# Local attention on one Trainium2 core: mask added by quarters of the array, values weighted right behind the scores, tokens transposed at a tile's end

## The reference

```python
def _layer(x, wqkv, qs, ksc, wo, lg, lb, w1, b1, w2, b2):
    h = shift_token(x)                       # second half of the features comes from the token before
    q, k, v = split(h @ wqkv)                # 8 heads of 64
    q = l2norm(q) * qs; k = l2norm(k) * ksc
    q, k = rotary_xpos(q, k)
    o = local_attention(q, k, v)             # windows of 64 queries, 128 keys: own window and the one before
    x = x + o @ wo
    h = layernorm(shift_token(x))
    a, g = split(h @ w1 + b1)
    return x + (a * gelu(g)) @ w2 + b2

# in local_attention
mask = (i < j) | (i > j + WINDOW) | (j == -1)
attn = softmax(where(mask, -max, 8 * q @ k.T))
```

## Time and profile before

| | |
|---|---|
| median of 3 runs | 3174.81 us (3174.18 to 3176.89) |
| profiled execution: its time, its span | 3177.26 us, 3175.5 us |
| TensorE matmul busy | 3081.3 us (97%) |
| TensorE weight load busy | 2208.4 us (70%) |
| VectorE busy | 2697.3 us (85%) |
| ScalarE busy | 2268.3 us (71%) |
| GpSimd busy | 1674.1 us (53%) |
| mean granted TensorE clock | 0.992 of full speed |
| chain that ended last | PE 92%, DVE 4%, issue 2%, ACT 1% |

### The profile page before, as it was taken

One profiled execution on the slowest core, in us unless ns is written; L12 is line 12 of the kernel. 1 busy time (PEld: TensorE's weight loads), 2 busy tenths in 40 slices (PEclk: granted clock), 3 DMA queues, 4 the chain that ended last, 5 costly groups with the idle time before them and its releaser, 6 DMA issues.

```text
span 3175.5 us, 83658 instructions
## 1 busy us (share of the span) xinstructions
PE 3081.3 (97%) x30466; PEld 2208.4 (70%) x30497; DVE 2697.3 (85%) x6053; ACT 2268.3 (71%) x5488; POOL 1674.1 (53%) x1000
## 2 busy tenths in 40 slices
PE   6999999999999999989999699999999999999999
PEld 3777777666777777657777477777766677777765
DVE  6999999678999888768999599999966889899865
ACT  4888888537888888328888388888853688888842
POOL 6788776215666565441000578878621466666610
PEclk9999999999999999999999799999999999999999
DMA  4111112201111112200000011111211111111211
GB/s 115 32 34 34 32 36 44 51 20 31 32 35 33 32 39 46 48 9 1 1 1 1 18 34 36 32 32 32 50 48 21 31 32 36 32 32 40 48 38 50
DMA packets 136852, 107.18 MB, mean 34 GB/s; under 512 B 80937, under 2 KB 102402, under 8 KB 136450
## 3 DMA queue, kind: packets, MB, share of 16 engines
q1 hardware_dynamic: 136450, 101.83, 14.2%
HBM read 12.67 MB, written 4.19 MB: 5 GB/s over the span
## 4 chain that ended last, share of the span: by engine, by line
PE 92%; DVE 4%; issue 2%; ACT 1%; DMA 0%; SPq 0%; DVEq 0%; ACTq 0%
PE psum L1172 15%; PE psum L1044 10%; PE psum L1149 7%; PE psum L1194 7%; PE psum L1216 7%; PE psum L1183 7%; PE psum L1101 7%; PE psum L1070 5%; PE psum L1135 4%; PE psum L1230 3%; PE psum L1243 3%; PE psum L1416 3%; PE psum L1392 3%; PE psum L1089 2%; PE psum L1125 2%
## 5 line engine op out<-in xcount | busy, mean ns | idle before, releaser
L421 POOL TENSOR_TENSOR rnorm<-ssq_floor,neg_half 128x16 f32<-128x16 f32 x256 | 746.3, 2915 | 725.3 <-DVE qkr L739 691.8
L426 POOL TENSOR_TENSOR qk_cos<-qk_cos,qk_sin 128x1024 f32<-128x1024 f32 x256 | 606.3, 2368 | 0.0
L496 ACT ACTIVATE shared<-psum,neg_max 128x128 f32<-128x128 f32 x2048 | 582.5, 377 | 27.1 <-DVE neg_max L715 27.0
L1172 PE MATMUL psum<-wqkv,hT 128*128 128x512 f32 x1024 | 558.0, 629 | 22.2 <-DVE qk_sin L700 9.7
L503 ACT ACTIVATE sq<-psum 128x512 f32<-128x512 f32 x512 | 318.2, 621 | 115.5 <-PE psum L1172 115.4
L700 DVE TENSOR_TENSOR qk_sin<-psum,sin 128x256 f32<-128x256 f32 x1024 | 381.7, 414 | 22.2 <-ACT sq L503 21.4
L556 ACT ACTIVATE shared<-psum,b1g 128x512 f32<-128x512 f32 (+1 forms) x192 | 131.2, 685 | 353.5 <-PE psum L1044 349.3
L706 DVE TENSOR_TENSOR qk_cos<-psum,cos 128x512 f32<-128x512 f32 x512 | 348.1, 681 | 13.5 <-ACT sq L503 13.3
L531 ACT COPY shared<-psum 128x512 f32<-128x512 f32 x512 | 276.4, 592 | 111.1 <-PE psum L1216 111.0
L715 DVE TENSOR_REDUCE neg_max<-psum 128x4 f32<-128x512 f32 x512 | 327.7, 682 | 31.5 <-PE psum L1103 29.7
L1044 PE MATMUL psum<-shared,w1g 128*128 128x512 f32 (+1 forms) x768 | 347.4, 596 | 7.2 <-DVE shared L805 5.3
(11 more groups left out here) (134 smaller groups left out, 6468.2 us busy)
## 6 DMA issues: line engine op xcount, KB each, us to landing
vprev<-v SPq DMA_DIRECT2D x512, 130.0 KB, 2.3
shared<-Y SPq DMA_DIRECT2D x32, 256.0 KB
shared<-Y SPq DMA_DIRECT2D x32, 254.0 KB
X<-in_L_attn_x SPq DMA_DIRECT2D x8, 512.0 KB, 6.9
out<-X SPq DMA_DIRECT2D x8, 512.0 KB, 3.5
wqkv<-in_L_ffn_wqkv SPq DMA_DIRECT2D x4, 768.0 KB, 4.4
w<-in_L_ffn_w SPq DMA_DIRECT2D x4, 341.0 KB
wo<-in_L_ffn_wo SPq DMA_DIRECT2D x4, 256.0 KB, 5.2
```

Source lines behind the costliest of these rows:

```text
L421: nc.gpsimd.tensor_tensor(rnorm[:], ssq_floor[:], neg_half[:], ALU.pow).then_inc(rnorm_ready, 1)
L426: nc.gpsimd.tensor_tensor(both, both, qk_sin[:, t.m % 2, :], ALU.add).then_inc(sum_ready, 1)
L496: last = nc.scalar.activation(probs[:, c * P:(c + 1) * P], bank(3 + i, (c % 4) * P, (c % 4 + 1) * P), ACT.Exp, bias=neg_max[:, c:c + 1])
L1172: nc.tensor.matmul(bank(i), hT[:, t.m * P:(t.m + 1) * P], wqkv[:, i * INNER:(i + 1) * INNER], start=True, stop=True).then_inc(qk_psum, 1)
```

## The change

1. The mask is added by four matmuls of 64 rows by 64 columns, in the same quarters of the array as the scores, for every tile. In a sequence's first tile the two quarters of the first window take the mask that closes the keys before it, the two of the second window the ordinary one; `ident16` is gone.
2. `weigh_values` comes right behind `scores`, ahead of `heads_transpose`.
3. `tokens_transpose` moves from behind the scores to the end of a step, behind the weights, one tile earlier in the pipeline's count (tile s+5 in step s), and writes bank 4, the second bank of the scores, once the exponents of step s are done. Tiles 0 to 4 of a layer are as before (bank 6 or 1).
4. ScalarE copies the tokens between the two halves of the weights instead of at the start of a step. The scores wait for this copy (`hT_ready`), since they write bank 4 again.

The diff:

```diff
--- before.py
+++ after.py
@@ -54,7 +54,7 @@
     i = np.arange(P)[:, None] % WIN
     j = np.arange(P)[None, :]
     open_ = (j >= i) & (j <= i + WIN)
-    first = open_ & ((np.arange(P)[:, None] >= WIN) | (j >= WIN))
+    first = open_ & (j >= WIN)
     return np.stack([np.tile(np.where(m, 0.0, MASKED), (1, 4)) for m in (first, open_)]).astype(np.float32)
 
 
@@ -136,7 +136,6 @@
         cos = sb("cos", [P, MT, 2, DH])
         sin = sb("sin", [P, MT, 2, DH])
         mask = sb("mask", [P, 2, BANK], BF16)
-        ident16 = sb("ident16", [P, P], BF16)
         windows16 = sb("windows16", [P, P], BF16)
 
         hT = sb("hT", [P, MT * P + 1])
@@ -285,7 +284,7 @@
             return ((2, 3), (4, 5), (0, 1))[c], 3
 
         def x_bank(t):
-            return 1 if t.L and t.row < 5 else 6
+            return 4 if t.row >= 5 else 1 if t.L else 6
 
         def v_bank(t):
             return 0 if t.L and t.row < 3 else 5
@@ -523,12 +522,11 @@
                     act.wait_ge(vprev_ready[u.m % 4], 32 * (u.n // 4 + 1))
                 nc.scalar.copy(v[:, t.m % 4, :, 0:DH], heads(bank(v_bank(t)))).then_inc(v_ready, 1)
 
-            def weights(t):
-                for i in range(2):
-                    cols = slice(i * BANK, (i + 1) * BANK)
-                    act.wait_ge(probsT_psum, 2 * t.n + i + 1)
-                    wait(act, pv_ready, before(t, 1))
-                    nc.scalar.copy(probsT[:, cols], bank(6 + i)).then_inc(probsT_ready, 1)
+            def weights(t, i):
+                cols = slice(i * BANK, (i + 1) * BANK)
+                act.wait_ge(probsT_psum, 2 * t.n + i + 1)
+                wait(act, pv_ready, before(t, 1))
+                nc.scalar.copy(probsT[:, cols], bank(6 + i)).then_inc(probsT_ready, 1)
 
             def rotated(t):
                 wait(act, scores_ready, before(t, 2))
@@ -557,7 +555,7 @@
                                      ACT.Gelu, bias=b1g[0:size, 1, c:c + 1]).then_inc(gate_ready, 1)
 
             def local_slot(L, s):
-                if t := tile_at(L, s + 4):
+                if s <= 0 and (t := tile_at(L, s + 4)):
                     tokens(t)
                 if t := tile_at(L, s - 2):
                     outputs(t)
@@ -578,7 +576,11 @@
                 if t := tile_at(L, s + 4):
                     squares(t, 1)
                 if t := tile_at(L, s):
-                    weights(t)
+                    weights(t, 0)
+                if s >= 0 and (t := tile_at(L, s + 5)):
+                    tokens(t)
+                if t := tile_at(L, s):
+                    weights(t, 1)
                 if t := tile_at(L, s + 2):
                     rotated(t)
                 if s == NT - 2:
@@ -996,7 +998,6 @@
             nc.vector.memset(h[0:1, :, 0, HALF:P], 0.0).then_inc(consts_done, 1)
             nc.vector.memset(hid2[:], 1.0).then_inc(consts_done, 1)
             dve.wait_ge(ident_in, 16)
-            nc.vector.tensor_copy(ident16[:], ident[:]).then_inc(consts_done, 1)
             for w in range(2):
                 nc.vector.tensor_tensor(windows16[:, w * WIN:(w + 1) * WIN], ident[:, 0:WIN], ident[:, WIN:P],
                                         ALU.add).then_inc(consts_done, 1)
@@ -1078,18 +1079,18 @@
                 wait(pe, kT_ready, before(t, 0, 2))
                 wait(pe, x1_ready, before(t, 3))
                 wait(pe, probs_ready, before(t, 1, 2))
+                if t.row and (u := tile_at(t.L, t.row + 4)):
+                    wait(pe, hT_ready, before(u, 0, 2))
                 if t.row == 0 and t.L == DEPTH:
                     pe.wait_ge(theta_ready, NT)
                     pe.wait_ge(pT_ready, 2 * NT)
                 elif t.row == 0:
                     wait(pe, hid_ready, 3 * NG * t.L)
-                for i in range(2):
-                    if t.m:
-                        rows = slice(WIN * i, WIN * i + WIN)
-                        nc.tensor.matmul(bank(3 + i), windows16[rows, :], mask[rows, 1, :],
-                                         start=True, stop=False, skip_group_check=True)
-                    else:
-                        nc.tensor.matmul(bank(3 + i), ident16[:], mask[:, 0, :],
+                for w in range(2):
+                    for i in range(2):
+                        rows, queries = slice(WIN * i, WIN * i + WIN), slice(WIN * w, WIN * w + WIN)
+                        nc.tensor.matmul(bank(3 + i, rows=queries), windows16[rows, queries],
+                                         mask[rows, 0 if w == 0 and t.m == 0 else 1, :],
                                          start=True, stop=False, skip_group_check=True)
                 lo = 0 if t.m else WIN
 
@@ -1110,10 +1111,10 @@
                     pe.wait_ge(ln_ready, 2 * NT * (t.L // DEPTH) + t.row + 1)
                 else:
                     pe.wait_ge(y_ready, (t.L - 1) * NG + t.row // GROUP + 1)
-                if x_bank(t) == 6 and t.row < 5:
+                if x_bank(t) == 6:
                     wait(pe, hT_ready, before(t, 1, 2))
-                elif x_bank(t) == 6:
-                    wait(pe, probsT_ready, 2 * (t.n - 5) + 1)
+                elif x_bank(t) == 4:
+                    wait(pe, probs_ready, 2 * (t.n - 4))
                 elif u := tile_at(t.L, t.row - 3):
                     wait(pe, qT_ready, before(u, 0))
                 elif t.row:
@@ -1210,8 +1211,6 @@
                         pe.wait_ge(b1_ready, 2 * t.L + 2)
                 elif i == 1:
                     wait(pe, o_ready, before(t, 1, 2))
-                elif u := tile_at(t.L, t.row + 4):
-                    wait(pe, hT_ready, before(u, 0, 2))
                 for c in range(4 * i, 4 * i + 4):
                     last = nc.tensor.transpose(bank(6 + i, (c % 4) * P, (c % 4 + 1) * P),
                                                probs[:, c * P:(c + 1) * P], ident[:])
@@ -1262,22 +1261,21 @@
                         combine(group_at(L - 1, NG - 1))
                     project_qk(tile(4), 0)
                     if L == 0:
-                        pe.wait_ge(consts_done, 10)
+                        pe.wait_ge(consts_done, 9)
                     scores(tile(0))
                     project_v(tile(3))
                     project_qk(tile(4), 1)
                     gate_offsets(L)
                     weights_transpose(tile(0), 0)
                     weights_transpose(tile(0), 1)
+                    tokens_transpose(tile(5))
                     keys_transpose(tile(2))
                     queries_transpose(tile(2))
                 elif s < NT:
                     scores(tile(0))
-                    if t := tile(4):
-                        tokens_transpose(t)
+                    weigh_values(tile(-1))
                     if t := tile(-2):
                         heads_transpose(t)
-                    weigh_values(tile(-1))
                     if t := tile(4):
                         project_qk(t, 0)
                     if t := tile(3):
@@ -1288,6 +1286,8 @@
                         project_out(t)
                     weights_transpose(tile(0), 0)
                     weights_transpose(tile(0), 1)
+                    if t := tile(5):
+                        tokens_transpose(t)
                     if t := tile(2):
                         keys_transpose(t)
                         queries_transpose(t)
```

## The result

The changed kernel takes **3250.77 us** (median of 4 runs, 3248.67 to 3253.07) against 3174.6 us before (median of 4, 3174.18 to 3176.89): 1.0239 times as long, 95% interval 1.0221 to 1.0256. The forecast was slower, 3255 us, range 3205 to 3275.

What follows compares the result with a forecast made beforehand. TensorE bounds the kernel at 8.55 us a step; the change closes a loop through ScalarE's query copy of 8.85. That gives +67 us, with the layers' ends and small terms +80: 3255 us, range 3205 to 3275.

Steps and rivals of the forecast that it cites:

- TensorE's own sum, 8.24: TensorE's instructions in one changed step add up to 8.24 us, 0.31 less than 8.55.
- The quarters run side by side: The four mask matmuls on TensorE run four abreast, 0.22 us for all; one behind the other would take 0.88.
- The query copy is late: ScalarE's last copy of a step, moved later, holds up the next weighted values; TensorE stands 0.54 us a step.
- Length of the loop, 8.85: Weighted values, heads, ScalarE's step, query copy, next values: 8.85 us a step with waits, against 8.55 before.
- two waits that lengthen it: V's projection waits for the heads' copy, and the tokens' copy for their transpose: loop 8.85 instead of 8.73 us.
- The two chains: Plain loop through all of ScalarE's step, 8.73 us; with V's wait and TensorE's order to the tokens, 8.85.
- V's wait: V's projection on TensorE waits for the heads' copy, whose bank it reuses: start at 2.50 instead of 2.43 us.
- Sum: 56 steps in each of four layers give +67 us; with first steps, step 59 and layer ends, +80 in total.
- ScalarE's small wait ahead of the tokens: Sign: ScalarE idles only about 0.1 us, ahead of the tokens' copies, between heads' copy and query copy.
- Gains until the next wait.: Taking work from TensorE gains only until another engine, or a loop through several, becomes the longest.
- fast rival: TensorE stays the bound, query copy in time, 8.24 or 8.31 us a step: about 3128 us; chance 10%.
- The rule on drains: Changing tiling mode drains TensorE; by that alone two of five changes of shape go and the kernel gets faster.

Runs made afterwards that it cites:

- the fastest one: The changed kernel with queries transposed and copied ahead of keys, the heads' copy behind the first exponents and V's projection last of three: 3107.49 us, ratio 0.9784.

## Why the prediction was right, point by point

- **TensorE's own sum, 8.24.** Right: 8.21 where nothing else binds. Single terms: mask to first score 0.25 against 0.22 taken; first to last score 0.77, where it was 0.83 in the earlier trace rows, a gain at the scores that I had left out.
- **The quarters run side by side.** Shown by the mask alone (-38 us) and by the rows above: four records within 0.41 us, and the first score 0.25 behind the first of them.
- **The query copy is late and the values wait for it.** Shown three ways: queries first, heads first, and the added copy. TensorE stood 208.88 - 208.35 = 0.53 us, with 0.20 for score and change of shape; 0.54 was forecast. The 236 waits are 59 in each layer, and each of them ended 0.10 us after a query copy.
- **Length of the loop, 8.85.** Measured 8.82. The start after the copy was 0.10, not the 0.14 of the earlier trace rows, which accounts for the 0.03 to within the rows' rounding. The stations came as forecast, counted from the values' start at 200.06: the tokens' transpose at 6.00 (forecast 5.98), their copy at 6.31 (6.29), the end of the query copy at 8.72 (8.71). The sum for 8.85 runs over V and TensorE's order to the tokens, yet the prediction named all of ScalarE's step as the loop, with two waits that lengthen it. That loop's own length is 8.73. The heads' copy moved later showed that the part through the exponents can be slack without any gain. The two chains differ by 0.12 us in the prediction's own sums, so the number was right while the name given to it was not.
- **V's wait.** It was forecast as V starting 0.07 late. V starts on time and costs 0.08 more, beside a weight load that starts only with it. The size was right for another reason, which was luck.
- **Sum.** 56 steps per layer from step 3 to 59 gave +14.3 to +14.6 us, +58 in all against +67 forecast: 0.04 us a step too much, 0.03 from the loop and 0.01 because I measured from 8.55, not from the mean 8.56. The ends of the layers gave +0.2 and +2.6 up to the last mask and +0.8 behind it, some +14.5 against +15; in this, step 59 was forecast at -1 in all and gave +0.6. The first steps, with -0.8 to +0.5 per layer, come to 0, and the stretches between the layers give back 1 to 2 us. Together 71 against 80 by the profiled executions, and 76 by the medians.
- **A sign that did not come.** VectorE's wait for the output projection was to grow. It shrank, from 94.4 us in 229 waits to 34.6 in 20 over the span; VectorE waits for ScalarE's squares instead (178.1 us, 230 times). ScalarE's small wait ahead of the tokens doesn't show either: the row before them (205.82) starts 0.56 after the squares instead of 0.49.
- **"Gains until the next wait."** The fast rival's 3128 us was what the change would do with the query copy in time; with the queries first it was 3132.75.
- **The rule on drains.** The Trainium skill, TensorEngine Tiling (Array Packing), Key Properties, says a change of tiling mode drains the engine. The runs agree that a change costs time: the kernel with the heads first has one change of shape more than the fastest one (four against three; its expectation counts two, wrongly), and its step is 8.40 - 8.21 = 0.19 us longer: 0.10 for the change and 0.10 for the projection that comes first behind it. The rule's forecast of a gain failed only because of the wait.

## What to carry to other kernels

Before two pieces of work are moved next to each other on the busiest engine, look at what the second waits for, and at how long before it that was ready: the work between them was its cover. Here 0.9 us of cover went for 0.3 us of work saved. Then write down the whole cycle, both ways: through the waiting engine's own order and through the other engine's. Shortening the one that isn't the longest gains nothing, even where, as here, they differ by only 0.12 us. An extra instruction of known length in the suspected chain, in both kernels, tells in one pair of runs whether it binds; put it into a stretch that only one of the chains has, or it can't tell them apart.

## What the runs showed of the hardware

- A float32 projection of 128 x 512 on the full array (two records) takes 0.86 us until the next start where its weights were loaded ahead, and about 0.1 more where the load starts only with the matmul. Three cases show it: behind a change of shape (0.97 in the earlier trace rows), behind a stand of 0.20 us (0.96 in the kernel with the tokens not moved), and for V, whose load waited although the array did not stand (0.94). In the whole trace of the changed kernel the single records with their load 0.1 us or more ahead follow each other after 0.43 us (some 1240 of them), those of V with the load only 0.02 ahead after 0.51.
- Four bfloat16 matmuls of 64 x 64 with 512 columns, one in each quarter of the array, cost 0.25 us together, from the first of them to the first score.
- A wait that a row puts down to "issue" can be a semaphore wait on another engine: 236 of them here ended 0.10 us after ScalarE's query copy, and all but 4 went away when that copy came earlier.
